# Split-operand projections in the fold of a decoder layer on one NeuronCore

## What is computed

```python
x = x + _L0_attn_ref(_layernorm(x), w_qkva, gamma)   # gated scan: q * scan(sigmoid(a), kv)
x = x + _L0_xattn_ref(_layernorm(x), context, Wq, Wkv, null_kv, Wout, ln_scale, ln_bias)
x = x + _L0_ffn_ref(_layernorm(x), w_gate, w_up, w_down)
# within _L0_xattn_ref
q = split_heads(x @ Wq)
k, v = split(context @ Wkv)          # 512 -> 2 x 1024
sim = (q * scale) @ concat(nk, k)^T
out = (softmax(sim) @ concat(nv, v)) @ Wout
out = layernorm(out, eps=1e-6) * ln_scale + ln_bias
```

## Time and profile before

| | |
|---|---|
| median of 3 runs | 495.75 us (495.35 to 496.26) |
| profiled execution, its own time | 493.31 us |
| its span | 491.5 us |
| busy share of TensorE, VectorE, ScalarE, GpSimd | 94%, 82%, 67%, 63% |
| granted TensorE clock, mean | 0.994 of full speed |
| the fold in it | from about 97 to 155 us |

### The profile page before, as it was taken

The page is one execution under the profiler, slowest core; times in us unless marked ns, Lnnn a source line. Parts: engine busy times, 40 slices in busy tenths (PEclk is TensorE's granted clock), DMA queues, the critical chain, the costliest instruction groups (busy, mean ns, idle before and its releaser), DMA issues.

```text
span 491.5 us, 7915 instructions
## 1 busy us (share of the span) xinstructions
PE 461.3 (94%) x2504; PEld 361.7 (74%) x2532; DVE 402.8 (82%) x882; ACT 329.0 (67%) x429; POOL 308.8 (63%) x465
## 2 busy tenths in 40 slices
PE   1999999999999999999999999999999999999673
PEld 0777888787677788777778777878878777786432
DVE  4689988974555688998989989899898998997785
ACT  4556644144544344898888888889788888887551
POOL 2234555741011478897788787787877878888860
PEclk9999999999999999999999999999999999999989
DMA  8997000240000000012131121212222121222243
GB/s 261 325 373 280 3 0 1 43 87 1 1 1 1 1 0 7 12 27 59 39 54 40 39 59 39 55 39 44 54 44 49 40 58 40 44 49 60 48 107 98
DMA packets 67129, 31.72 MB, mean 65 GB/s; under 512 B 49680, under 2 KB 65296, under 8 KB 67088
## 3 DMA queue, kind: packets, MB, share of 16 engines
q1 hardware_dynamic: 67088, 31.21, 25.2%
HBM read 15.21 MB, written 4.19 MB: 39 GB/s over the span
## 4 chain that ended last, share of the span: by engine, by line
PE 83%; DVE 6%; POOL 5%; issue 2%; DMA 2%; ACT 2%; SPq 0%; POOLq 0%; DVEq 0%; ACTq 0%
PE psum L1285 37%; PE psum L1301 12%; PE psum L1564 10%; PE psum L1559 10%; PE psum L1536 3%; PE psum L1544 2%; PE psum L1389 2%; PE psum L1425 2%; PE psum L1406 2%; PE psum L1320 2%; PE psum L1336 1%; DMA gcol<-in_L_attn_gamma_dram 1%; DVE region_a L1008 1%; DVE region_c L1111 1%; PE psum L1556 1%
## 5 line engine op out<-in xcount | busy, mean ns | idle before, releaser
L577 POOL TENSOR_TENSOR region_d<-region_d,rden 128x1024 f32<-128x1024 f32 x30 | 57.1, 1904 | 13.4 <-DVE rden L1087 13.1
L1559 PE MATMUL psum<-VW,region_d 128*128 128x256 f32 x256 | 60.6, 380 | 0.2
L1564 PE MATMUL psum<-VW,region_d 128*128 128x256 f32 x256 | 60.5, 379 | 0.0
L1071 DVE TENSOR_REDUCE mx<-psum 128x8 f32<-128x512 f32 x64 | 44.0, 687 | 14.3 <-PE psum L1285 13.2
L1285 PE MATMUL psum<-Mhi,xT2hi 128*128 128x512 f32 x128 | 53.8, 420 | 0.7 <-DVE xT2lo L1053 0.6
L1564 PEld LDWEIGHTS psum<-VW,region_d 128*128 128x128 f32 x256 | 48.6, 190 | 6.6
L1111 DVE SCALAR_TENSOR_TENSOR region_c<-psum,hzw,region_c 128x1024 f32<-128x1024 f32 x32 | 41.1, 1283 | 12.9 <-ACT region_c L791 12.7
L1559 PEld LDWEIGHTS psum<-VW,region_d 128*128 128x128 f32 x256 | 46.3, 190 | 6.5 <-ACT region_d L862 0.6
L1285 PE MATMUL psum<-Mhi,xT2lo 128*128 128x512 f32 x128 | 50.3, 393 | 0.0
L1285 PE MATMUL psum<-Mlo,xT2hi 128*128 128x512 f32 x128 | 50.0, 390 | 0.0
L1076 DVE SCALAR_TENSOR_TENSOR region_d<-mx,psum 128x512 f32<-128x512 f32 x60 | 40.9, 681 | 1.0
(11 more groups left out here) (160 smaller groups left out, 1164.3 us busy)
## 6 DMA issues: line engine op xcount, KB each, us to landing
out_dram<-xs SPq DMA_DIRECT2D x32, 128.0 KB, 1.9
xs<-in_x_dram SPq DMA_DIRECT2D x1, 2560.0 KB, 13.2
VW<-in_L_xattn_Wkv_dram SPq DMA_DIRECT2D x1, 2048.0 KB, 12.9
region_b<-in_L_xattn_Wkv_dram SPq DMA_DIRECT2D x1, 2048.0 KB, 16.8
xs<-in_x_dram SPq DMA_DIRECT2D x3, 512.0 KB, 6.7
region_w<-in_L_ffn_w_gate_dram SPq DMA_DIRECT2D x2, 512.0 KB, 9.6
region_w<-in_L_ffn_w_up_dram SPq DMA_DIRECT2D x2, 512.0 KB, 7.8
region_w<-in_L_ffn_w_down_dram SPq DMA_DIRECT2D x8, 128.0 KB, 5.7
```

What stands on the lines that cost most here:

```text
L577: pool.tensor_tensor(p_of(t).rearrange("p (h j) -> p h j", j=MK), e[:, :, 0:MK], rden[:, v, :].unsqueeze(2).broadcast_to([P, H, MK]), ALU. ...
L1071: dve.tensor_reduce(mx[:, hh, :], scores, AX.X, ALU.max).then_inc(max_done, 1)
L1559: pe.matmul(bank(7, D), pT[:, pair, :], VW[:, batch(n), pair, :], start=False, stop=False)
L1564: mm = pe.matmul(bank(7, D), pT[:, pair, :], VW[:, batch(n), pair, :], start=False, stop=pair == HC - 1)
```

## The change

Each projection becomes three groups of four fp32r products: high weights with high context, high weights with low context, low weights with high context. ScalarE's copy of the context gives the high half, a new VectorE subtraction from the same PSUM banks the low half. The weight slice of each projection is split by GpSimd (split_kvw): a copy to fp32r, then a subtraction, into two slots, so that split i waits for projection i - 2. The halves lie in xT1hi and xT1lo, free after stage 1. Splits 0 and 1 stand behind the last rounding, 2 and 3 ahead of the last two power operations of the second norm, 4 to 9 each ahead of an addition of wsum, 10 to 13 behind them, 14 and 15 between the probabilities of tiles 0 and 1. The exponentials of tiles 0 and 1 move into the second half of VW, wsum into its last piece, and the probabilities of tiles 0 and 1 into the two slots of region_d; their multiplication is made in two halves. So the evictions of fold_values(2), on VectorE and on ScalarE, wait for both probabilities. ScalarE's wait for the transposes of the first two MLP weights moves from ahead of the first kvT eviction to ahead of the first Mhi eviction. The left-out hunks declare four semaphores (ctxT_lo_ready, kvw_hi, kvw_ready, p_first) and adapt views of e_of.

```diff
--- before.py
+++ after.py
@@ -160,19 +160,23 @@
         w1 = a["y"][:, 0:KD * 3 * D].rearrange("p (k n) -> p k n", k=KD)
         c = carve(region_c, [("sg", FI), ("h", FI), ("n", 2 * D // 2),
-                             ("nq", FI // 2), ("nhT", FI // 2), ("wsum", D)])
-        wsum = c["wsum"]
+                             ("nq", FI // 2), ("nhT", FI // 2)])
         hid3 = [c["sg"], c["h"]]
         n3 = c["n"].bitcast(BF16).rearrange("p (r d) -> p r d", r=2)
         f = carve(region_b, [("wq", KD * INNER), ("wout", HC * D), ("ctx", 2 * CTX),
-                             ("wv", CC * INNER), ("ctxT", CC * BM),
+                             ("wv", CC * INNER), ("gap", CC * BM),
                              ("kvT", 4 * BM)])
         wq_raw = f["wq"].rearrange("p (k n) -> p k n", k=KD)
         wout = f["wout"].rearrange("p (c n) -> p c n", c=HC)
         ctx_raw = f["ctx"].rearrange("p (r n) -> p r n", r=2)
         wv = f["wv"].rearrange("p (k n) -> p k n", k=CC)
-        ctxT = f["ctxT"].rearrange("p (k n) -> p k n", k=CC)
+        xT1hi_flat = xT1hi[:, :, :, :].rearrange("p r k n -> p (r k n)")
+        xT1lo_flat = xT1lo[:, :, :, :].rearrange("p r k n -> p (r k n)")
+        ctxThi = xT1hi_flat[:, 0:CC * BM].rearrange("p (k n) -> p k n", k=CC)
+        kvwhi = xT1hi_flat[:, CC * BM:].rearrange("p (r k n) -> p r k n", r=2, k=CC)
+        kvwlo = xT1lo_flat[:, 0:CC * BM].rearrange("p (r k n) -> p r k n", r=2, k=CC)
+        ctxTlo = xT1lo_flat[:, CC * BM:].rearrange("p (k n) -> p k n", k=CC)
         kvT = f["kvT"].rearrange("p (r n) -> p r n", r=4)
         yTs = f["kvT"].rearrange("p (t d) -> p t d", t=GT)
         COPIED = 5
@@ -198,8 +202,8 @@
         s = carve(region_d, [("y", 2 * D), ("z", 2 * D), ("nT", 2 * D // 2), ("nh", FI // 2), ("free", D),
-                             ("xn", 4 * D), ("e", 2 * H * J), ("p", 2 * H * MK), ("pT", HC * P),
-                             ("nhT", FI // 2)])
+                             ("xn", 4 * D), ("e", 2 * H * J), ("nhT", FI // 2), ("gap", 480),
+                             ("p", 2 * H * MK), ("pT", HC * P)])
         xn2 = s["xn"].rearrange("p (r d) -> p r d", r=4)
         e2 = s["e"].rearrange("p (r n) -> p r n", r=2)
         p2 = s["p"].rearrange("p (r n) -> p r n", r=2)
...
@@ -360,15 +368,17 @@
             return isinstance(n, int) and 0 <= n < 5
-        early = region_c[:, 0:2 * H * J + H * MK]
+        late_pairs = VW[:, :, HC // 2:, :].rearrange("p b c n -> p b (c n)")
+        wsum = VW[:, B - 1, HC - 1, :]
         def e_of(t):
-            return early[:, t * H * J:(t + 1) * H * J] if t < 2 else e2[:, t % 2, :]
+            return late_pairs[:, 2 * t:2 * t + 2, 0:HB * J] if t < 2 else \
+                e2[:, t % 2, :].rearrange("p (r n) -> p r n", r=2)
         def p_of(t):
-            return early[:, 2 * H * J:] if t == 0 else p2[:, t % 2, :]
+            return p2[:, 1 - t % 2, :]
         def score_bank(t):
@@ -522,8 +532,23 @@
                 pool.wait_ge(magic_added, i + 1)
                 pool.tensor_scalar(raw[i], raw[i], 1.0, -MAGIC, ALU.mult, ALU.add).then_inc(round_done, 1)
+            def split_kvw(i):
+
+                w = (wk if i < HC else wv)[:, :, (i % HC) * P:(i % HC + 1) * P]
+                pool.wait_ge(wk_loaded if i < HC else wv_loaded, 16)
+                if i == 0:
+                    pool.wait_ge(q_psum, NG)
+                if i > 1:
+                    pool.wait_ge(fT_psum, i - 1)
+                pool.tensor_copy(kvwhi[:, i % 2, :, :], w).then_inc(kvw_hi, 1)
+                pool.wait_ge(kvw_hi, i + 1)
+                pool.tensor_tensor(kvwlo[:, i % 2, :, :], w, kvwhi[:, i % 2, :, :].bitcast(F32), ALU.subtract) \
+                    .then_inc(kvw_ready, 1)
+
             def stage1(g, u):
+                if g == NG or g == NG + 1:
+                    split_kvw(g - NG + 2)
                 if exists(g + 2, NG):
                     pool.wait_ge(pw_in_set, 2 * (g + 2) + 2)
                     pool.tensor_tensor(pw_out[:, :], pw_in[:, :], expo[:, :], ALU.pow).then_inc(pw_done, 1)
@@ -544,17 +569,22 @@
                     rounded(1)
                 if isinstance(g, int) and g == NG - 1:
                     rounded(2)
+                    split_kvw(0)
+                    split_kvw(1)
             groups(stage1)
             pool.wait_ge(nvsel_zero, 1)
             for row in (0, DH // 2):
                 pool.tensor_copy(nvsel[:, row:row + 1], nulls[:, 1:2]).then_inc(nv_set, 1)
             pool.wait_ge(wout_loaded, 16)
-            pool.wait_ge(q_psum, NG)
             pool.tensor_tensor(wsum, wout[:, 0, :], wout[:, 1, :], ALU.add).then_inc(wout_summed, 1)
             for pair in range(2, HC):
+                split_kvw(pair + 2)
                 pool.wait_ge(wout_summed, pair - 1)
                 pool.tensor_tensor(wsum, wsum, wout[:, pair, :], ALU.add).then_inc(wout_summed, 1)
+            for i in range(HC + 2, HC + 6):
+                split_kvw(i)
+
             def add_output(t):
                 v = t % 2
@@ -569,14 +599,22 @@
                 v = t % 2
                 pool.wait_ge(rden_done, t + 1)
-                if t == 1:
-                    pool.wait_ge(fT_psum, 2 * HC)
                 if t > 1:
                     pool.wait_ge(pT1_psum, t - 1)
-                e = e_of(t).rearrange("p (h j) -> p h j", j=J)
-                pool.tensor_tensor(p_of(t).rearrange("p (h j) -> p h j", j=MK), e[:, :, 0:MK],
-                                   rden[:, v, :].unsqueeze(2).broadcast_to([P, H, MK]), ALU.mult) \
-                    .then_inc(p_ready, 1)
+                if t < 2:
+                    if t == 1:
+                        pool.wait_ge(kvw_ready, 2 * HC)
+                    for hh in range(2):
+                        heads = slice(hh * HB, (hh + 1) * HB)
+                        pool.tensor_tensor(p_of(t).rearrange("p (h j) -> p h j", j=MK)[:, heads, :],
+                                           e_of(t)[:, hh, :].rearrange("p (h j) -> p h j", j=J)[:, :, 0:MK],
+                                           rden[:, v, heads].unsqueeze(2).broadcast_to([P, HB, MK]), ALU.mult) \
+                            .then_inc(*((p_ready, 1) if hh == 1 else (p_first, 1)))
+                else:
+                    e = e2[:, v, :].rearrange("p (h j) -> p h j", j=J)
+                    pool.tensor_tensor(p_of(t).rearrange("p (h j) -> p h j", j=MK), e[:, :, 0:MK],
+                                       rden[:, v, :].unsqueeze(2).broadcast_to([P, H, MK]), ALU.mult) \
+                        .then_inc(p_ready, 1)
             def cast_h(t):
@@ -627,7 +665,7 @@
             def stages2_3(n, u4):
                 if exists(n - 1, T):
                     add_output(n - 1)
-                if exists(n + 1, T):
+                if n > 0 and exists(n + 1, T):
                     probabilities(n + 1)
                 if n == T - 1:
                     deviation4(n - 2)
@@ -643,6 +681,9 @@
                         quantise_z(n - 3)
             probabilities(0)
+            split_kvw(2 * HC - 2)
+            split_kvw(2 * HC - 1)
+            probabilities(1)
             pool.wait_ge(ln_loaded, 32)
             steps(stages2_3)
@@ -704,7 +745,7 @@
                 if isinstance(g, int) and g == NG - 1:
                     act.wait_ge(ctxT_psum, 1)
-                    act.activation(ctxT.rearrange("p k n -> p (k n)"), banks(0, 2).rearrange("p b n -> p (b n)"),
+                    act.activation(ctxThi.rearrange("p k n -> p (k n)"), banks(0, 2).rearrange("p b n -> p (b n)"),
                                    ACT.Copy).then_inc(ctxT_ready, 1)
@@ -721,9 +762,6 @@
             act.activation(wqT[:, 0:HC // 2, :].rearrange("p c n -> p (c n)"),
                            banks(2, 2).rearrange("p b n -> p (b n)"), ACT.Copy, scale=DH ** -0.5) \
                 .then_inc(wqT0_ready, 1)
-            act.wait_ge(wT_ready[0], 16)
-            act.wait_ge(wT_ready[1], 16)
-
             def put_kvT(i):
@@ -736,6 +774,9 @@
             def put_keys_hi(i):
+                if i == 0:
+                    act.wait_ge(wT_ready[0], 16)
+                    act.wait_ge(wT_ready[1], 16)
                 act.wait_ge(fold_psum, i + 1)
                 for half_ in range(2):
                     at = slot_of(2 * i + half_) * MK
@@ -747,6 +788,8 @@
                 if q == 0:
                     act.wait_ge(wT_ready[2], 16)
+                if q == 2:
+                    act.wait_ge(p_ready, 2)
                 act.wait_ge(fold_psum, HC + q + 1)
                 for half_ in range(2):
                     act.activation(VW[:, 2:4, 2 * q + half_, :], bank(3 + 2 * half_).rearrange("p (b n) -> p b n", b=2),
...
@@ -1008,6 +1052,10 @@
                     dve.tensor_tensor(y1[:, u, :, :], banks(2, 2), hid[:, u, :, :], ALU.mult) \
                         .then_inc(y1_done, 1)
                 if isinstance(g, int) and g == NG - 1:
+                    dve.wait_ge(ctxT_ready, 1)
```

(38 more changed lines are left out.)

## The result

The changed kernel takes 496.77 us (median of 20 runs, 495.03 to 499.11) where the kernel before takes 495.20 (20 runs of the same comparison): a ratio of 1.0039, 95% interval 1.0027 to 1.0051. It is slower by 1.3 to 2.5 us. I had predicted 495.8 us and no change, with 0.35 on slower. Measured against it the change is clearly slower, and the likeliest case did not come true. The profiled execution took 496.26 us, its span 494.4.

A forecast was written before the change was run, and what follows sets the result against it. TensorE, 83% of the span, bounds the kernel. Cheaper projections save up to 4.6 us, but the late fold start and waits leave fold_values(3) 0.1 earlier: 495.8 us, no change, range 494.2 to 498.3.

The forecast's parts named there:

- the likeliest case: Whole kernel: 495.8 us, no change, own range 494.8 to 496.8; chance 0.43.
- the one row of that width: 256-column product of ones_r and vnull on TensorE: 0.12 us a step, so 1.44 for a projection's twelve products.
- the signs of a right forecast: In the fold: key pairs about 2.7 us, fold_keys(0) at 107 to 108, subtraction near 1.28, fold_values(3) within 0.5 of 153.
- the exclusion of VectorE and GpSimd: Start of the fold: the two engines block each other, priced at 0.9 us between bounds of 0 and about 4.
- My reason for the low price: Start of the fold: blocking pieces are short beside the gaps between VectorE operations that suffer, hence 0.9 us.
- slower by the lock: Start of the fold: ternary passes and small operations each wait for a subtraction; price near 3 us, 497.9 total; chance 0.20.
- the pairs gave back: Key half up to fold_keys(7): five pairs, each 0.28 us shorter, give back 1.4 us.
- the value half gives back little: Late fold: savings of kv_T(11) to (15) mostly end in waits; fold_values(3) starts only 0.1 us earlier than before.
- the wait for the probabilities: Evictions of fold_values(2) wait for the second probabilities, taking up the 0.9 us that kv_T(13) to (15) save.
- GpSimd's pace and TensorE's are alike: Key half: GpSimd needs 2.70 us a pair, TensorE 2.69, so both run at nearly one pace.
- the moved wait for the transposes is free: ScalarE's wait, moved to the first Mhi eviction behind 107.10: the transpose at 105.4 is early enough, costing nothing.

The follow-up runs named there:

- no_early_low: The changed kernel without GpSimd's subtractions of splits 0 to 3, those third product groups repeating the high weights; ratio 0.9995 to the kernel before.
- scores_first: The changed kernel with tile 1's scores ahead of fold_values(1) and its softmax and exponential ahead of those evictions; ratio 0.9994 to the kernel before.
- before_scores_first: The kernel before, plain projections, with tile 1's scores ahead of fold_values(1) and its softmax ahead of those evictions; ratio 0.9995 to the kernel before.
- start_reordered: The changed kernel with both ternary passes, the last power operation and its shift, and Wout's additions moved at the fold's start; ratio 0.9959 to the kernel before.
- power_first: The changed kernel with the splits of the third and fourth pair behind the two last power operations; ratio 1.0080 to the kernel before.
- ternary_first: The changed kernel with w_up's ternary pass ahead of the context's subtraction on VectorE; ratio 0.9986 to the kernel before.
- both_reordered: The changed kernel with the reordered fold start and tile 1's scores and softmax moved ahead; median 492.28 us, ratio 0.9936 to the kernel before.
- no_context_low: The changed kernel without VectorE's subtraction for the context's low half, the second product group repeating the high context; ratio 1.0021 to the kernel before.
- both_again: The same kernel as both_reordered, run once more; median 491.87 us, ratio 0.9936 to the kernel before.

## Why the prediction was right or wrong

The prices of the single operations held. A split was 0.61 + 0.08 + 1.28 (forecast 0.60 + 0.09 + 1.28), the multiplication in two halves 2.06 (2.1), a projection 1.63 behind the 64-row products (1.44 + 0.19), the pair 2.69. A projection without a restart took 1.44 us, twelve products at 0.12, as the one row of that width had said. The Trainium skill ("FP8 and Floating Point Precision", "TensorE Precision Notes") has four passes for a true fp32 product and truncates the operands of the reduced form to the native precision, which I read as one pass; twelve would then take 1.30, an estimate, and the measurement stands against it. kv_T(0) was forecast 0.8 late and is 0.8 late. fold_keys(0), the pair and the subtraction came as the signs of a right forecast had them. fold_values(3) did not: it was to lie within 0.5 us of 153 and starts at 154.57, 154.36 less the later start of all.

The step that failed is the exclusion of VectorE and GpSimd: I took 0.9 us between bounds of 0 and 4, and it is 1.97 on the way to the last variance sum, as no_early_low measures: two small shifts (1.10 and 0.63), the variance sum L963 (0.13) and a ternary pass (0.11). With the 1.92 by which the passes start later, that makes 3.89; the trace has the sum 3.90 later (110.33 against 106.22, less 0.21 for the later start of all). The forecast was 2.9. The fifth split started 3.76 later instead of 2.9, and fold_keys(2) 2.87 late instead of 1.8. My reason for the low price, that the pieces are short beside the gaps, was wrong: from 97.73 to 108.52 us GpSimd left none of more than about 0.1 us, and each blocked operation delays what collides next. So the outcome is the rival "slower by the lock" in its mechanism, with a price right at the point of 2.0 from which I had it decide, and two thirds of the price at which I had costed it. That 495.8 came within 1 us of the measured time says nothing for the mechanism: the start was priced 1.1 us too low, and nothing later made up for the difference, as that rival says. The lock for whole instructions that the Trainium skill describes ("SBUF — State Buffer", "Who interferes with whom") is what the rows show: L963, of which no row of before spoke, ended with the subtraction it met (104.44 and 104.41), and the passes that read PSUM did not wait (1.21 and 1.23 us).

Smaller misses: the pairs gave back 1.24 instead of 1.4, 0.27 of it lost to a wait that I had not seen, at 127.51, ahead of kv_T(9) behind pair_T. It ends with ScalarE's projection eviction, which stands behind four norm operations in ScalarE's queue; that cause is read from the timelines, no run took it away. And between fold_keys(7) and fold_values(1) nothing was recovered where I had 0.2.

Right was that the value half gives back little: of the 1.4 us that kv_T(11) to (15) save 0.25 arrived. But the wait for the probabilities took less of it than I had said. TensorE's waits ahead of fold_values(1), (2) and (3) are

```profile
141.22 1.96 PE L1464 MATMUL psum<-region_b 64*64 64x256 f32 x32 [0.69 <-ACT region_b L772]
...
149.28 1.96 PE L1464 MATMUL psum<-region_b 64*64 64x256 f32 x32 [0.29 <-issue]
...
154.57 1.96 PE L1464 MATMUL psum<-region_b 64*64 64x256 f32 x32 [0.88 <-ACT region_b L772]
```

where they were 0.10, none and 0.61 us: 0.59, 0.29 and 0.27 more. I had 0.4 for the first and 0.9, all that kv_T(13) to (15) save, for the last, behind the probabilities. The middle one ends with the eviction of kv_T(13), which stands behind the exponential of tile 1 in ScalarE's queue; that is read from the timeline and not tested. scores_first fills these waits, and before_scores_first, with 0.16 us, shows that they are new. Right too that GpSimd's pace and TensorE's are alike and neither a danger, that the moved wait for the transposes is free (the first Mhi eviction, at 109.18, is released by TensorE and by no DMA), and that nothing of size changes behind the fold: from tile 0 to the last tile the changed kernel takes 0.2 us more.

The change thus did what it says and saved TensorE 4.1 us of work; the start of the fold cost 2.87 on the path, and 1.24 and 0.25 came back. In the order of start_reordered the same products make a gain.

## What to carry to other kernels

When work is taken from the bounding engine and given to others, look first at where the new work must begin: the loss here lay in the first 15 us, where two engines that exclude each other were both dense, and a pace well inside the budget later did not repay it. Count a blocked operation's cost along the chain it is in, once for each meeting, and move what nobody waits for (a ternary pass, a sum, the last power operation) out of that stretch before the new work goes in. A saving behind a wait for another engine is only had when something else is put into the wait.

## What the runs showed of the hardware

TensorE's clock fell to its lower level after short waits. In power_first it was granted 0.51 behind 2.07 us of idle, in ternary_first behind 1.29; in the changed kernel, with waits of 0.84, 1.48 and 1.30, and in start_reordered, with 1.32, it stayed at 1.00, and in both profiles of both_reordered too, behind 1.29 and 1.30. The lower level cost 1.4 and 1.3 us for the twelve products behind the wait. Waits of 1.29 and 1.3 us stand on both sides, so the length of the wait alone does not decide it; what does stays open.

The stretch from the last tile's first product to the end varied, with nothing edited there: 37.4 us in no_early_low, 37.7 before, 38.8 in the changed kernel, 41.2 in no_context_low. The windows 475 to 485 and 485 to 490 of no_early_low,

```profile
475.00:485.00 10.00, 6.66 (x45) 3.99 (x45) 8.73 (x19) 4.21 (x4) 2.08 (x2) 0.98 0.57 126
485.00:490.00 5.00, 2.52 (x24) 1.68 (x21) 1.55 (x4) 0.60 (x1) 0.00 (x0) 1.00 0.21 72
```

and of no_context_low,

```profile
475.00:485.00 10.00, 8.74 (x44) 4.98 (x44) 6.52 (x13) 4.52 (x4) 2.08 (x2) 0.77 0.47 111
485.00:490.00 5.00, 3.06 (x19) 1.92 (x17) 2.88 (x8) 0.60 (x1) 0.00 (x0) 0.64 0.44 106
```

show the granted clock at 0.98 and 1.00 in the one, 0.77 and 0.64 in the other, although the stretch is at like stages in both. TensorE is in use 8.74 us in the first window of no_context_low and 6.66 in that of no_early_low, for 44 and 45 products. Other executions point the same way: of the six of both_again the two slowest (494.31 and 494.58 us) have the lowest mean clocks (0.984 and 0.987), and the fastest (490.67) has 0.995. That is why a profile's span (495.3 and 491.0 here) says less of such an edit than the distances inside it. What makes the clock fall there in one execution and not in the next stays open.
